# Experts by lists of tokens, weight rows loaded ahead, and the down weights turned inside the attention stage before

## The chip, the cores and the metric

One core of one Trainium2 chip runs the whole program. The metric is device time in microseconds (us); lower is better. The kernel before was timed in three runs.

## The reference, cut to what matters

Two layers, each an attention-like block and a feed-forward block, on `x` of 4 sequences of 512 tokens with 128 features (2048 tokens). The parts that the change touches are the last two: the relative-position attention of the second layer, and its mixture of 8 experts, of which each token uses the one with the largest router logit.

```python
def _L1_ffn_ref(x, router_w, expert_fc, expert_proj):     # E = 8, D = 128, HD = 512
    logits = jnp.einsum('btd,ed->bte', x, router_w)
    probs = jax.nn.softmax(logits, axis=-1)
    expert_ids = jnp.argmax(probs, axis=-1)
    mask = jax.nn.one_hot(expert_ids, E, dtype=x.dtype)
    h = jnp.einsum('btd,edh->ebth', x, expert_fc)
    h = jnp.square(jax.nn.relu(h))
    out_e = jnp.einsum('ebth,edh->ebtd', h, expert_proj)
    return jnp.einsum('ebtd,bte->btd', out_e, mask)
...
x = x + ga * _L1_attn_ref(h, ...)                          # relative attention
h = _layernorm(x, axis=-1) * (1 + cb) + sb
x = x + gb * _L1_ffn_ref(h, L1_ffn_router_w, L1_ffn_expert_fc, L1_ffn_expert_proj)
```

## The kernel before, in words

The program is a row of stages (test-time layer, six transformer layers, relative attention, experts); at the end of each, `end_phase` makes all five engines meet. Inside a stage every engine has its own hand-written order of instructions, and semaphores (`Signal`) tie them: `x.by(event)` raises, `x.on(event)` is waited for. An engine that waits holds everything behind it in its own order. DMAs issued by SP (SyncE) go through one queue, indirect DMAs (row numbers taken from a tile) are issued by POOL (GpSimd), one per 128 rows.

**Relative attention.** 256 tiles of 8 queries are worked through in rounds (`relative_rounds`), two tiles a round: `score_tiles` (L1878, L1884) on PE, the largest score on DVE (L2028), the exponential on ACT (L1996), a turn of the weights by PE one round later (L1899), and a copy of the turned tiles out of PSUM in `relative_keep` (L1952), the even tile on ACT, the odd one on DVE. The next round's scores wait for these copies, since the PSUM banks go round by five. From round 9 on PE also sums the values (L1921, L1931). POOL builds the masked query rows for every four rounds (`make_rows`, L2040 and L2049), and SP fetches them (`fetch_rows`). `t.xc` and `t.hT` of this stage are used only by its early part.

**Experts.** All 2048 tokens are sorted into tiles of 128 that belong to one expert each: `TILES` = 16 + 8 - 1 = 23, of which the last of each expert is partly filled and some may be empty. In order:

- A norm (L256 to L303). Between its two halves PE turns the router and, in `turn_expert` (L2197), all down weights `expert_proj`; DVE and ACT copy them out (L2318, L2279) and SP writes them beside the up weights into a table in memory of 1024 rows of 4 KB (`t.table`). SP also clears `t.sorted`.
- Router logits (L2217), h turned to rows by token (L2221), counts of tokens before each token (`counts_tensor`, L2265 to L2270), the gates (L2225), x turned to rows by token (L2230).
- `places_vector` on DVE (L2360 to L2376): the sorted row of each token (`at_i`), then the weight rows of each tile (`row_i`).
- POOL scatters h into `t.sorted`, 16 indirect DMAs (L2395). SP loads the sorted rows back (L2180). POOL gathers the weights, 23 indirect DMAs of 512 KB into 6 buffers (L2403), each from the seventh on waiting for `downed` of the tile six before.
- The tile loop: PE turns the tile (L2239), up (L2248), relu on DVE (L2338), square on ACT (L2299), down (L2257), copy out on ACT (L2305), store to `t.answers` by SP (L2183).
- When all tiles are stored, POOL gathers the answers back by token, 16 indirect DMAs (L2408); DVE multiplies by the gate and adds x (L2344, L2346) for every four, and SP stores the result (L2187).

The lines that set the order around the change:

```python
G.wait_ge(*t.placed.on(0)); G.wait_ge(*t.zero_in.on(0))
for m in range(NT): ...                      # 16 scatters of h, L2395
for n in range(TILES):
    if n >= WEIGHTS:                         # WEIGHTS = 6
        G.wait_ge(*t.downed.on(n - WEIGHTS))
    G.e.indirect_dma_start(out=t.w[n % WEIGHTS], in_=t.table, ...)     # L2403
for y_out in t.y_out: G.wait_ge(*y_out.all())
for m in range(NT): ...                      # 16 gathers of answers, L2408
```

Of the kernel before, what the change touches and what calls it, by code (L numbers as in the profile page):

```python
# [7 lines left out]
F32 = mybir.dt.float32  # L8
BF16 = mybir.dt.bfloat16
# [153 lines left out]
def setup(nc, io, whole):  # L163
# [8 lines left out]
    c.xT = sbuf(c, whole, "xT", [P, B, S])  # L172
    c.modT = sbuf(c, whole, "modT", [P, 2, 6, B])
# [1401 lines left out]
SPLIT_FROM = len(UNITS) - 2  # L1575
SUM_AT = {"heads": 8, "spread": 8, "out": 8, "turn": 9, "scale": 10, "back": 11, "add": 14, "o_turn": 15, "o_copy": 16, "mix": 16, "bias": 17}
# [197 lines left out]
def relative_late_setup(c, t, scope):  # L1774
# [20 lines left out]
    t.q_made, t.q_high, t.q_low = (Signal(nc, "rel_q_" + n, halves) for n in ("made", "high", "low"))  # L1795
    t.q_shared, t.sums_zeroed = Signal(nc, "rel_q_shared", [0]), Signal(nc, "rel_sums_zeroed", [0])
# [47 lines left out]

def relative_sync(c, t):
# [10 lines left out]
    for signal in (*t.qd_in, *t.o_out.values(), *t.o_in.values()):  # L1856
        SP.wait_ge(*signal.all())
# [30 lines left out]
def relative_tensor(c, t):  # L1888
    PE, psum, ident = c.PE, c.psum, c.ident
    for r, at, valued in relative_rounds():  # L1890
# [4 lines left out]
        if p is not None:  # L1895
            for n in (2 * p, 2 * p + 1):
# [3 lines left out]
                last.then_inc(*t.turned.by(n))  # L1900
        for u, k in valued:
# [33 lines left out]
            if k == SUM_AT["turn"]:  # L1935
# [3 lines left out]
                PE.wait_ge(*t.v_kept.all())  # L1939
# [21 lines left out]
def relative_scalar(c, t):  # L1961
    A = c.A
    for r, at, valued in relative_rounds():
        for u, k in valued:
# [152 lines left out]
LOADS = [range(i, min(i + 4, TILES)) for i in range(0, TILES, 4)]  # L2117
WEIGHTS, UP_LAG, DOWN_LAG = 6, 1, 3


def experts_setup(c, scope):
# [4 lines left out]
    t.table, t.sorted, t.answers = dram("expert_table", (NE * P, 2 * HD)), dram("sorted_tokens", (TILES * P, P)), dram("sorted_answers", (TILES * P, P))  # L2126
# [17 lines left out]
    t.const_in, t.pr_in = Signal(nc, "router_in", range(3), 16), [Signal(nc, f"pr_in{e}", [0], 16) for e in experts]
    t.fc_in, t.pr_out, t.zero_in = Signal(nc, "fc_copied", [0], 16), Signal(nc, "pr_out", experts, 16), Signal(nc, "zeros_in", [0], 16)
    t.zeroed, t.numbered = Signal(nc, "experts_zeroed", [0]), Signal(nc, "experts_numbered", [0])
# [304 lines left out]
```

## Time and profile before

| what | us |
|---|---|
| time, median of 3 runs (lowest, highest) | 2559.96 (2552.66, 2569.27) |
| the profiled execution: its time | 2556.95 |
| the profiled execution: its span | 2555.2 |
| PE busy | 2367.3 (93%) |
| DVE busy | 1749.7 (68%) |
| ACT busy | 1600.4 (63%) |
| POOL busy | 1477.4 (58%) |
| experts stage, from its first instruction to the end of the span | 2415.0 to 2555.2 |

The span goes from the first to the last instruction of the profiled execution; 1.75 us of its time lie outside. Times below are microseconds from the span's start. "Granted clock" is TensorE's clock as a share of its upper level. An engine's idle time costs only where the chain of waits passes through it.

### The profile page before, as it was taken

Reading aid. Unit: us, or ns where it says so; the run is one execution under the profiler, and the core shown is the slowest. Engines: PE = TensorE matmul, PEld = TensorE weight load, DVE = VectorE, ACT = ScalarE, POOL = GpSimd, SP = SyncE. Lnnn points to the kernel's source line nnn. Section 1 sums busy time; section 2 is a strip of 40 time slices with the busy share of each in tenths; the row PEclk is TensorE's granted clock in tenths of the full one; section 3 lists DMA queues with packets and bytes.
Section 4 is the critical chain, followed back from the end, with each engine's and each line's share of the span. In section 5 each row is a group of like instructions: output and inputs, shape, how many; then the busy total and the mean of one; then the engine's idle time right before and its main releaser. Section 6 shows DMA issues by size and latency. Waiting matters only on the chain.

```text
span 2555.2 us, 121984 instructions
## 1 busy us (share of the span) xinstructions
PE 2367.3 (93%) x53661; PEld 1739.5 (68%) x53661; DVE 1749.7 (68%) x3521; ACT 1600.4 (63%) x5055; POOL 1477.4 (58%) x1452
## 2 busy tenths in 40 slices
PE   9858999999999999999999999999889999999855
PEld 8736777777777777777777777777546666666654
DVE  4497887888878888888888877887345555555422
ACT  3226777777777777777777777777534454454322
POOL 1156676666766676667766676664137665566144
PEclk9979999999999999999999999999979999999967
DMA  4013333333333334333343333333132222222255
GB/s 90 14 32 81 80 83 95 91 82 83 94 90 88 85 83 95 93 85 83 93 95 80 86 91 80 89 85 85 36 78 51 47 47 47 48 47 47 69 193 166
DMA packets 234111, 203.55 MB, mean 80 GB/s; under 512 B 133720, under 2 KB 160230, under 8 KB 233454
## 3 DMA queue, kind: packets, MB, share of 16 engines
q1 hardware_dynamic: 227070, 181.28, 29.2%
q0 software_dynamic: 4336, 14.16, 1.7%
q8 instruction: 422, 6.91, 1.2%
q14 instruction: 107, 0.88, 0.1%
q10 hardware_dynamic: 2176, 0.33, 0.1%
HBM read 84.09 MB, written 16.15 MB: 39 GB/s over the span
## 4 chain that ended last, share of the span: by engine, by line
PE 68%; DVE 16%; issue 5%; POOL 3%; SPq 3%; DMA 3%; ACT 2%; POOLq 0%; ACTq 0%; DVEq 0%
PE psum L1197 8%; PE psum L1215 5%; PE psum L1223 5%; PE psum L1899 5%; PE psum L1098 5%; PE psum L1878 4%; PE psum L1884 3%; PE psum L1100 3%; PE psum L1099 3%; PE psum L1931 3%; DVE kT L1430 3%; PE psum L1921 3%; DVE rotated L1405 3%; PE psum L1174 2%; PE psum L1205 2%
## 5 line engine op out<-in xcount | busy, mean ns | idle before, releaser
L1342 ACT ACTIVATE p<-p,stat 128x64 f32<-128x64 f32 x1536 | 512.3, 336 | 38.2 <-DVE stat L1477 36.2
L1560 POOL TENSOR_TENSOR p<-p,inverse 128x512 f32<-128x512 f32 x192 | 200.3, 1043 | 461.6 <-DVE inverse L1480 460.4
L1197 PE MATMUL psum<-kT,qT 32*32 32x64 f32 x24576 | 305.5, 223 | 27.3 <-issue 25.9
L1197 PEld LDWEIGHTS psum<-kT,qT 32*32 32x32 f32 x24576 | 263.5, 103 | 78.1 <-issue 76.8
L2028 DVE TENSOR_REDUCE largest<-psum 128x1 f32<-128x512 f32 x256 | 164.9, 686 | 221.5 <-PE psum L1884 221.5
L1405 DVE SCALAR_TENSOR_TENSOR rotated<-psum,scales,rotary 128x512 f32<-128x512 f32 x384 | 271.5, 742 | 26.3 <-ACT sq L1278 26.0
L1342 ACT ACTIVATION_READ_ACCUMULATOR p<-p,stat 128x1 f32 x1536 | 289.1, 188 | 0.0
L1539 POOL TENSOR_TENSOR sq<-sq 128x512 f32<-128x512 f32 x192 | 245.3, 1277 | 46.6 <-ACT sq L1278 46.5
L1278 ACT ACTIVATE sq<-psum 128x512 f32<-128x512 f32 x384 | 213.0, 582 | 68.6 <-PE psum L1128 52.3
L1952 ACT ACTIVATE w_by_key<-psum 128x512 f32<-128x512 f32 x128 | 76.5, 597 | 245.0 <-PE psum L1899 245.0
L1215 PEld LDWEIGHTS psum<-pT,v_win 64*64 64x64 f32 x12288 | 197.0, 135 | 48.0 <-issue 40.7
L1098 PE MATMUL psum<-xs,wqkv_high 128*128 128x512 f32 x384 | 206.4, 537 | 18.8 <-DVE rotated L1405 13.0
L1215 PE MATMUL psum<-pT,v_win 64*64 64x32 f32 x12288 | 218.4, 220 | 1.8 <-ACT pT L1348 1.4
L1223 PEld LDWEIGHTS psum<-oT,wo 128*128 128x128 f32 x1536 | 187.6, 196 | 41.4 <-issue 30.9
L1223 PE MATMUL psum<-oT,wo 128*128 128x128 f32 x1536 | 198.6, 283 | 12.1 <-issue 6.8
L1348 ACT ACTIVATE pT<-psum 128x512 f32<-128x512 f32 x192 | 114.3, 595 | 140.0 <-PE psum L1205 139.9
L1291 ACT ACTIVATE v_tok<-psum 128x512 f32<-128x512 f32 x192 | 114.0, 594 | 95.7 <-PE psum L1100 79.7
L2040 POOL TENSOR_TENSOR q_by_head<-q_heads,mask_head 64x256 fp32r<-64x256 f32 x252 | 157.4, 624 | 15.4
L1996 ACT ACTIVATE weights<-psum,largest 128x512 f32<-128x512 f32 x256 | 161.5, 687 | 3.5 <-DVE largest L2028 3.5
L1546 POOL TENSOR_TENSOR qT<-qT,rotated 128x512 f32<-128x512 f32 x96 | 162.9, 1697 | 0.0
L1430 DVE TENSOR_TENSOR kT<-kT,rnorm_wide 128x1024 f32<-128x1024 f32 x96 | 157.6, 1642 | 3.5 <-DMA rnorm_wide<-rnorms 3.4
L1405 DVE SCALAR_TENSOR_TENSOR kT<-psum,scales,rotary 128x512 f32<-128x512 f32 x192 | 141.9, 739 | 22.2 <-ACT sq L1278 19.8
(344 smaller groups left out, 5488.2 us busy)
## 6 DMA issues: line engine op xcount, KB each, us to landing
v_win<-v_tok SPq DMA_DIRECT2D x576, 128.0 KB
rnorm_wide<-rnorms SPq DMA_DIRECT2D x384, 64.0 KB
v_win<-v_tok SPq DMA_DIRECT2D x336, 64.0 KB
q_rows<-q_rows_all SPq DMA_DIRECT2D x32, 512.0 KB, 4.7
wqkv<-L_ffn_Wqkv SPq DMA_DIRECT2D x96, 64.0 KB, 2.4
rel_values<-sq SPq DMA_DIRECT2D x60, 64.0 KB, 2.2
wo<-L_ffn_Wo SPq DMA_DIRECT2D x48, 64.0 KB
wqkv<-L_ffn_Wqkv SPq DMA_DIRECT2D x12, 256.0 KB, 2.9
```

Source lines behind the costliest of these rows:

```text
L1098: PE.e.matmul(out, w[0], x[1], start=True, stop=False)
L1197: last = PE.e.matmul(psum[WIN * blk:WIN * (blk + 1), f, out], q[rows, g, half, tok:tok + WIN], k[rows, g, half, tok:tok + 2 * WIN], start= ...
L1215: last = PE.e.matmul(psum[to:to + DH, 2 + o, at:at + WIN], v[rows, blk, 2 * (2 * a + o) + h, :], t.pt[h][rows, 2 * a + o, blk * WIN:(blk + ...
L1223: last = PE.e.matmul(ps[:, 0:P], t.wo[:, e, :], t.ot[e % 2][:, e // 2, :], start=(e == 0), stop=(e == PAIRS - 1))
L1278: A.e.activation(t.sq[half][:, :], c.psum[:, 4 + half, :], ACT.Square).then_inc(*t.squared.by((u, (p, half))))
L1342: last = A.e.activation(p, p, ACT.Exp, bias=t.stat[:, h, 2 * g + f:2 * g + f + 1], accum_out=t.sum[:, h, g, f:f + 1])
L1405: last = V.e.scalar_tensor_tensor(out=rot[x], in0=psum[:, 4 + half, :], scalar=scale, in1=table, op0=ALU.mult, op1=ALU.mult)
L1430: V.e.tensor_tensor(k, k, t.wide[g % 2][:, :].unsqueeze(1).to_broadcast([P, 2, S]), ALU.mult).then_inc(*t.k_scaled.by((u, g)))
L1539: G.e.tensor_tensor(t.sq[0][:, :], t.sq[0][:, :], t.sq[1][:, :], ALU.add).then_inc(*t.squares.by((u, p)))
L1546: G.e.tensor_tensor(second, second, t.turned_by[1][:, :], ALU.add).then_inc(*t.made.by((u, p)))
L1560: G.e.tensor_tensor(p, p, t.inv[:, h, :, :].unsqueeze(3).to_broadcast([P, GROUPS_TF, 2, 2 * WIN]), ALU.mult).then_inc(*t.p_scaled.by(m))
L2028: V.e.tensor_reduce(t.mx[n % 4][:, :], psum[:, n % 5, :], AX, ALU.max, negate=True).then_inc(*t.largest.by(n))
```

## The change

**Relative attention.** The table of weights becomes part of the whole program (`c.table`). SP starts the copy of the up weights into it as its first step of the rounds. In rounds 1 to 8 SP loads the down weights of one expert into `t.xc` (`fetch_weights`), in rounds 4 to 11 PE turns one expert's (four transposes into PSUM bank 7, behind the turn of that round's tiles and ahead of the value sums) and ACT copies it out (ahead of its `relative_keep`), and in rounds 6 to 13 SP stores it (`store_weights`).

**Experts.** The turning and the clearing are gone. Rows of (h, x, gate), 1536 bytes for each of the 2048 tokens and one row of zeros, are written to memory by 13 plain DMAs of SP (`t.rows`). PE makes the gates before it turns h. `places_vector` now makes the weight rows first, and behind the sorted places it makes, with bitwise operations, comparisons and 16 small matmuls (`list_tensor`), a list of token numbers for each tile. SP loads each tile's weights by a plain DMA from a row number that it reads into a register (10 buffers). POOL issues 12 gathers of token rows, then a scatter of a finished tile straight into the output and a gather in turn, then the last 12 scatters; there is no way back over `t.answers`. Gate and x are applied per tile on DVE.

```diff
-WEIGHTS, UP_LAG, DOWN_LAG = 6, 1, 3
+WEIGHTS, LOOK, UP_LAG, DOWN_LAG = 10, 12, 1, 3
+NO_TOKEN = NT * P
...
+def fetch_weights(c, t, e):
+    SP = c.SP
+    SP.wait_ge(*c.norms["normed"].on((2, B - 1)))
+    if e >= 4:
+        SP.wait_ge(*t.pr_turned.on(e - 4))
+    SP.e.dma_start(t.xc[:, e % 4, :], c.io["L1_ffn_expert_proj"][e]).then_inc(*t.pr_in[e % 4].by(e))
...
+def store_weights(c, t, e):
+    SP.wait_ge(*t.pr_kept.on(e))
+    SP.e.dma_start(c.table[e * P:(e + 1) * P, HD:2 * HD], t.hT[:, e % 4, :]).then_inc(*t.pr_out[e % 4].by(e))
...
+def turn_weights_down(c, t, e):
+    PE.wait_ge(*t.v_kept.all())
+    PE.wait_ge(*t.pr_in[e % 4].on(e))
+    if e:
+        PE.wait_ge(*t.pr_kept.on(e - 1))
+    for j in range(TPB):
+        last = PE.e.transpose(c.psum[:, 7, j * P:(j + 1) * P], t.xc[:, e % 4, j * P:(j + 1) * P], c.ident[:, :])
+    last.then_inc(*t.pr_turned.by(e))
...
+def keep_weights_down(c, t, e):
+    A.wait_ge(*t.projected.on((B - 1, "v")))
+    A.wait_ge(*t.pr_turned.on(e))
+    if e >= 4:
+        A.wait_ge(*t.pr_out[e % 4].on(e - 4))
+    A.e.activation(t.hT[:, e % 4, :], c.psum[:, 7, :], ACT.Copy).then_inc(*t.pr_kept.by(e))
...
 def relative_sync(c, t):
+    SP.e.dma_start(c.table[:, 0:HD], c.io["L1_ffn_expert_fc"].rearrange("e d h -> (e d) h")).then_inc(*t.fc_in.by(0))
     for r, at, valued in relative_rounds():
+        if 0 <= r - TABLE_FIRST + TABLE_FETCH < NE:
+            fetch_weights(c, t, r - TABLE_FIRST + TABLE_FETCH)
+        if 0 <= r - TABLE_FIRST - TABLE_LAG < NE:
+            store_weights(c, t, r - TABLE_FIRST - TABLE_LAG)
...
 def experts_sync(c, t):
+    for b in range(B):
+        SP.e.dma_start(part(b, 2), t.gates[:, b:b + 1, :].to_broadcast([P, TPB, P])).then_inc(*t.rows_out.by(("g", b)))
+    for name, kept, source, j in (("h", t.h_kept, t.htok, 0), ("x", t.x_kept, t.xtok, 1)):
+        for b in range(B):
+            SP.wait_ge(*kept.on(b))
+            SP.e.dma_start(part(b, j), source[:, b * TPB:(b + 1) * TPB, :]).then_inc(*t.rows_out.by((name, b)))
+    SP.wait_ge(*t.rowed.on(0))
     for n in range(TILES):
-        SP.wait_ge(*t.y_kept.on(n))
-        SP.e.dma_start(t.answers[n * P:(n + 1) * P, :], t.y[n % 4][:, :]).then_inc(*t.y_out[n % 4].by(n))
+        row = SP.e.value_load(t.row_i[0:1, n:n + 1], min_val=0, max_val=(NE - 1) * P)
+        if n >= WEIGHTS:
+            SP.wait_ge(*t.downed.on(n - WEIGHTS))
+        SP.e.dma_start(t.w[n % WEIGHTS][:, :], c.table[bass.ds(row, P), :]).then_inc(*t.w_in[n % WEIGHTS].by(n))
...
+def list_tensor(c, t):
+    PE, lists = c.PE, c.psum[:, 6, 0:2 * TILES]
+    PE.wait_ge(*t.placed.on(0))
+    for m in range(NT):
+        last = PE.e.matmul(lists, t.in_slot[:, m, :], t.ids[:, m, :, :].rearrange("p j t -> p (j t)"), start=(m == 0), stop=(m == NT - 1))
+    last.then_inc(*t.listed.by(0))
...
 def places_vector(c, t):
-    V.e.tensor_copy(t.at_i[:, :], t.at[:, :]).then_inc(*t.placed.by(0))
+    then(V.e.tensor_copy(t.at_i[:, :], t.at[:, :]))
+    V.e.tensor_scalar(t.slot[:, :], t.at_i[:, :], P - 1, None, ALU.bitwise_and)
+    then(V.e.tensor_scalar(t.base[:, :], t.at_i[:, :], -P, None, ALU.bitwise_and))
+    by_tile = [P, NT, TILES]
+    then(V.e.tensor_tensor(t.in_tile[:, :, :], t.base[:, :].unsqueeze(2).to_broadcast(by_tile), t.tile_at[:, :].unsqueeze(1).to_broadcast(by_tile), ALU.is_equal))
+    V.e.tensor_tensor(t.ids[:, :, 0, :], t.in_tile[:, :, :], t.id_high[:, :].unsqueeze(2).to_broadcast(by_tile), ALU.mult)
+    V.e.tensor_scalar(t.ids[:, :, 1, :], t.in_tile[:, :, :], t.id_low[:, 0:1], None, ALU.mult)
+    by_slot = [P, NT, P]
+    V.e.tensor_tensor(t.in_slot[:, :, :], t.slot[:, :].unsqueeze(2).to_broadcast(by_slot), t.slot_n[:, :].unsqueeze(1).to_broadcast(by_slot), ALU.is_equal).then_inc(*t.placed.by(0))
+    V.wait_ge(*t.listed.on(0))
+    then(V.e.tensor_reduce(t.raw[:, :], psum[:, 6, 0:2 * TILES].rearrange("p (j t) -> p t j", t=TILES), AX, ALU.add))
+    V.e.tensor_scalar(t.token_i[:, :], t.raw[:, :], float(NO_TOKEN), None, ALU.add).then_inc(*t.tokens.by(0))
...
 def experts_vector(c, t):
+            V.e.tensor_tensor(t.y[:, n, :], psum[:, 4 + n % 2, 0:P], t.xs[:, n, 2 * P:3 * P], ALU.mult).then_inc(*t.gated.by(n))
+            V.wait_ge(*t.gated.on(n))
+            V.e.tensor_tensor(t.y[:, n, :], t.y[:, n, :], t.xs[:, n, P:2 * P], ALU.add).then_inc(*t.added.by(n))
...
 def experts_pool(c, t):
+    G.wait_ge(*t.tokens.on(0))
+    G.wait_ge(*t.rows_out.all())
+    out = c.io["out"].rearrange("b s d -> (b s) d")
+    for r in range(TILES + LOOK):
+        n = r - LOOK
+        if n >= 0:
+            G.wait_ge(*t.added.on(n))
+            G.e.indirect_dma_start(out=out, out_offset=bass.IndirectOffsetOnAxis(ap=t.token_i[:, n:n + 1], axis=0), in_=t.y[:, n, :], in_offset=None,
+                                   bounds_check=NO_TOKEN - 1, oob_is_err=False).then_inc(*t.stored.by(n))
+        if r < TILES:
+            G.e.indirect_dma_start(out=t.xs[:, r, :], out_offset=None, in_=t.rows, in_offset=bass.IndirectOffsetOnAxis(ap=t.token_i[:, r:r + 1], axis=0),
+                                   bounds_check=NO_TOKEN).then_inc(*t.xs_in[r % (LOOK + 1)].by(r))
```

## Rows read from the trace of the kernel before

**Rows 1.** the page: the chain that ended last, by engine

```profile
PE 68%; DVE 16%; issue 5%; POOL 3%; SPq 3%; DMA 3%; ACT 2%; POOLq 0%; ACTq 0%; DVEq 0%
```

**Rows 2.** windows: length, busy PE PEld DVE ACT POOL, granted clock, DMA share, GB/s

```profile
2440.00:2442.00 2.00, 2.00 (x11) 2.00 (x12) 1.45 (x5) 0.60 (x1) 0.00 (x0) 0.50 0.03 8
...
2460.00:2480.00 20.00, 4.99 (x22) 4.61 (x23) 1.02 (x2) 1.29 (x4) 13.06 (x14) 0.50 0.52 183
2480.00:2500.00 20.00, 19.77 (x170) 18.86 (x168) 7.29 (x11) 9.60 (x30) 8.98 (x9) 1.00 0.94 297
...
2520.00:2540.00 20.00, 4.02 (x33) 3.72 (x32) 2.84 (x5) 2.04 (x6) 9.84 (x10) 0.70 0.21 58
```

**Rows 3.** groups by line, 2411-2556 us: count, busy us, mean ns, idle before

```profile
L2403 POOL DMA_INDIRECT tile_weights<-expert_table,weight_row_i x23 | 23.1, 1002 | 24.0 <-PE psum L2257 15.6 <-issue 8.3
...
L2408 POOL DMA_INDIRECT y_tokens<-sorted_answers,row_at_i x16 | 16.7, 1043 | 15.9 <-DMA sorted_answers<-tile_y 11.3 <-issue 4.6
...
L2395 POOL DMA_INDIRECT sorted_tokens<-h_tokens,row_at_i x16 | 15.8, 989 | 33.8 <-DVE row_at_i L2370 29.2 <-issue 4.6
...
L2372 DVE TENSOR_TENSOR past<-tile_number,end 128x184 f32<-128x184 f32 x1 | 0.3, 344 | 0.0
```

**Rows 4.** timeline, head of the experts stage: start us, us, engine, line

```profile
2426.29 0.18 DVE L225 SCALAR_TENSOR_TENSOR rstd<-root_t,rstd 128x16 f32<-128x16 f32 x1
...
2432.63 3.74 PE L268 MATMUL psum<-ident,rstd 128*128 128x128 f32 x32
...
2440.22 3.65 PE L2221 MATMUL psum<-ident,hT 128*128 128x128 f32 x16
...
2443.88 1.03 PE L2270 MATMUL psum<-chosen,all_ones 128*128 128x120 bf16 x15
...
2444.77 1.70 PE L2225 MATMUL psum<-ident,gate 128*128 128x128 f32 x8
...
2447.61 0.18 DVE L2370 CAST row_at_i<-row_at 128x16 int32<-128x16 f32 x1
...
2448.71 1.24 POOL L2395 DMA_INDIRECT sorted_tokens<-h_tokens,row_at_i  x1 [29.23 <-DVE row_at_i L2370]
...
2474.76 0.66 PE L2239 MATMUL psum<-ident,sorted_x 128*128 128x128 f32 x2 [26.55 <-DMA sorted_x<-sorted_tokens]
```

**Rows 5.** timeline, end of the experts stage

```profile
2524.70 0.28 ACT L2305 ACTIVATE tile_y<-psum 128x128 f32<-128x128 f32 x1 [0.77 <-PE psum L2257]
...
2539.27 1.52 POOL L2408 DMA_INDIRECT y_tokens<-sorted_answers,row_at_i  x1 [0.30 <-issue]
2539.93 0.69 DVE L2346 TENSOR_TENSOR y_tokens<-y_tokens,x_tokens 128x512 f32<-128x512 f32 x1
...
2547.66 1.01 POOL L2408 DMA_INDIRECT y_tokens<-sorted_answers,row_at_i  x1 [0.30 <-issue]
...
2551.01 0.69 DVE L2346 TENSOR_TENSOR y_tokens<-y_tokens,x_tokens 128x512 f32<-128x512 f32 x1
```

**Rows 6.** timeline, first rounds of the relative attention

```profile
1919.26 0.96 PE L1878 MATMUL psum<-keys,q_by_head 64*128 64x512 f32 x6 [0.25 <-ACT w_by_key L1952]
...
1920.75 1.09 PE L1899 MATMUL psum<-ident,weights 128*128 128x128 f32 x8
...
1921.44 0.60 ACT L1952 ACTIVATE w_by_key<-psum 128x512 f32<-128x512 f32 x1 [1.07 <-PE psum L1899]
...
1922.09 0.96 PE L1878 MATMUL psum<-keys,q_by_head 64*128 64x512 f32 x6 [0.25 <-ACT w_by_key L1952]
...
1929.80 1.04 PE L1878 MATMUL psum<-keys,q_by_head 64*128 64x512 f32 x6 [2.30 <-POOL q_by_query L2049]
...
1934.08 0.97 PE L1878 MATMUL psum<-keys,q_by_head 64*128 64x512 f32 x6
...
1937.83 0.96 PE L1878 MATMUL psum<-keys,q_by_head 64*128 64x512 f32 x6
```

**Rows 7.** the page, DMA issues: KB each, us to landing

```profile
q_rows<-q_rows_all SPq DMA_DIRECT2D x32, 512.0 KB, 4.7
```

More of the change, by code:

```diff
@@ L2144, in experts_setup @@
[L2144 to L2146 removed]
+    t.place, t.at, t.at_i, t.slot, t.base = sb("place", [P, NT, NE]), sb("row_at", [P, NT]), sb("row_at_i", [P, NT], I32), sb("slot", [P, NT], I32), sb("tile_base", [P, NT], I32)
@@ L2160, in experts_setup @@
+    t.turned, t.kept, t.upped, t.relued, t.squared, t.downed, t.gated, t.added = (Signal(nc, "tile_" + n, tiles) for n in ("turned", "kept", "up", "relu", "square", "down", "gated", "added"))
+    t.stored = Signal(nc, "out_stored", tiles, 16, fresh=True)
     t.norm = Norm(c, 3, t.hT, c.xT, t.xc, c.modT[:, 1, 4, :], c.modT[:, 1, 3, :])
@@ L2177, in experts_sync @@
-    SP.wait_ge(*t.scattered.all())
-    for i, tiles in enumerate(LOADS):
-        rows = t.sorted[tiles[0] * P:(tiles[-1] + 1) * P, :].rearrange("(t p) d -> p t d", p=P)
-        SP.e.dma_start(t.xs[:, tiles[0]:tiles[-1] + 1, :], rows).then_inc(*t.xs_in[i].by(0))
-    for n in range(TILES):
-        SP.wait_ge(*t.y_kept.on(n))
-        SP.e.dma_start(t.answers[n * P:(n + 1) * P, :], t.y[n % 4][:, :]).then_inc(*t.y_out[n % 4].by(n))
-    out = io["out"].rearrange("b (c p) d -> p (b c) d", p=P)
@@ L2219, in experts_tensor @@
     for b in range(B):
+        last = PE.e.matmul(psum[:, 7, b * P:(b + 1) * P], c.gate[:, 1, 1, b:b + 1].to_broadcast([P, P]), c.ident[:, :], start=True, stop=True)
+    last.then_inc(*t.gate_out.by(0))
+    for b in range(B):
         for k in range(TPB):
@@ L2224, in experts_tensor @@
     for b in range(B):
-        last = PE.e.matmul(psum[:, 7, b * P:(b + 1) * P], c.gate[:, 1, 1, b:b + 1].to_broadcast([P, P]), c.ident[:, :], start=True, stop=True)
-    last.then_inc(*t.gate_out.by(0))
-    for b in range(B):
         PE.wait_ge(*t.h_kept.on(b))
@@ L2276, in experts_scalar @@
     norm_scalar(c, t.norm)
-    for e in range(1, NE, 2):
-        A.wait_ge(*t.pr_turned.on(e))
-        A.e.activation(t.prT[:, e, :], psum[:, 5, :], ACT.Copy).then_inc(*t.pr_kept[1].by(e))
+    A.wait_ge(*t.gate_out.on(0))
+    A.e.activation(t.gates[:, :, :].rearrange("p b d -> p (b d)"), psum[:, 7, :], ACT.Copy).then_inc(*t.gate_kept.by(0))
     for b in range(B):
@@ L2405, in experts_pool @@
-    for y_out in t.y_out:
-        G.wait_ge(*y_out.all())
-    for m in range(NT):
-        G.e.indirect_dma_start(out=t.ytok[:, m, :], out_offset=None, in_=t.answers, in_offset=bass.IndirectOffsetOnAxis(ap=t.at_i[:, m:m + 1], axis=0),
-                               bounds_check=TILES * P - 1).then_inc(*t.gathered[m // TPB].by(m % TPB))
+        last = G.e.memset(t.up_to[:, e, 0:e + 1], 1.0)
+    last.then_inc(*t.numbered.by(0))
+    G.wait_ge(*t.tokens.on(0))
+    G.wait_ge(*t.rows_out.all())
```

160 lines of the change are left out of this document (59 added, 101 removed).

## The prediction

> **What bounds the kernel now.** I read the chain of waits first. Over the whole span it runs mostly through PE [rows 1], so a stage that keeps PE full pays for every instruction added there. The experts stage is another case, which only windows show: while POOL scatters h, PE is busy 5 of 20 us at granted clock 0.50 (the lower level, 1.2 GHz); while the tiles are worked it is busy 19.8 of 20 at the upper one, with the DMA engines at 0.94; while POOL gathers the answers it is busy 4 of 20 [rows 2]. The groups say why: an indirect DMA holds POOL about 1.0 us and the next comes 0.3 us later. There are 16 + 23 + 16 = 55 of them [rows 3], 16 of them alone before the loop and 16 alone behind it. Last I read the timeline of the stage's two ends [rows 4, 5] and of the attention's first rounds, where work is put in [rows 6].
>
> **Experts, head.** The root of the norm is ready at 2426.47, yet the spread begins at 2432.63, because PE turns the down weights in between [rows 4]. That goes: the spread can begin 6.1 us earlier. PE then starts at its lower clock; I take 0.7 us of the gain back, so the logits end 5.4 us earlier, 2440.2 - 5.4 = 2434.8 (ends: 3 and 6.1). Next on PE came the turn of h (3.65), a short counting part and the counts (together to 2444.9, that is 4.7 after the logits). Now the gates go first, +1.70 [rows 4], so the counts end at 2434.8 + 4.7 + 1.7 = 2441.2. The clock was at its lower level during the turn of h [rows 2]; were it at the upper, this part would be some 2.5 us shorter, which I keep as a bound.
>
> DVE's old way from the counts to `at_i` took 2447.79 - 2444.91 = 2.9 us [rows 4]. Ahead of `at_i` now come the weight rows, three dependent operations: 0.38 + 0.38 + 0.2 = 1.0. Behind it: two bitwise ones of 16 columns, 0.4; then operations of 368, 368, 368 and 2048 columns. From 184 columns at 0.344 [rows 3] and 512 at 0.69 [rows 5] a column costs 1.05 ns over 0.15 us, so 0.54 + 0.54 + 0.54 + 2.3 = 3.9. The list is 16 small matmuls; 15 of the nearest kind took 1.03 [rows 4], so 1.3 with both hand-overs (not above 3). Two more operations, 0.5, and POOL starts 0.92 after DVE's end, as at 2448.71 after 2447.79 [rows 4]. Sum behind the counts: 2.9 + 1.0 + 0.4 + 3.9 + 1.3 + 0.5 + 0.9 = 10.9. POOL's first gather begins at 2441.2 + 10.9 = 2452.1, which is 3.4 us later than its first scatter today. POOL also waits for the 13 plain writes of rows (3 MB). Their last is issued about 5 us behind the counts (turn of x up to 3.7 at the lower clock, 0.6 on ACT). At the 297 GB/s of a full window [rows 2] the 3 MB take 10.6 us from 2437.4, where the gates are ready, so about 2449 and 2 us of landing: just covered. If they are slower by 2 us, they set the start.
>
> **Experts, loop and end.** POOL now issues 23 gathers and 23 scatters: 46 against 55. The gather's price per start is 1.0 + 0.3 = 1.31 us for 512 KB as for 64 KB, the scatter's 1.28 [rows 3, 4]; so size does not matter and 1536 bytes a row should cost 1.31 too. From the first start to the last: 23 x 1.31 + 22 x 1.28 = 58.3 us. That POOL sets the pace needs a comparison with the tiles. Tile 0 today is finished 8 us after its first turn, and all 23 take 2524.98 - 2474.76 = 50.2 us [rows 4, 5]. With 3.5 us for the first gather's landing, tile 22 is added about 54.5 us after POOL's start, the last scatter begins 58.3 after it, and the first at 12 x 1.31 = 15.7 against tile 0's 12. POOL is late by 4 us at both ends, so PE's loop is hidden under POOL and not the other way. DVE takes two more operations of 0.3 per tile and ACT loses one of 0.26; both have free time [rows 2].
>
> The last scatter lands 2.5 us after its start (DVE's work on the last gather begins that much behind 2547.66 [rows 5]) and the span ends 0.3 later. So the span would end at 2452.1 + 58.3 + 2.8 = 2513.2, not at 2555.2: 42.0 us earlier. Gone are the 16 scatters ahead (20 us), the reload (6), the 16 gathers behind (21) and the way out (8); come back 3.4 at the start and the loop's stretch from 50 to 61.
>
> SP's plain weight loads hide here: the weight rows are known 2441.2 + 3.9 = 2445, the h and x writes are ahead of them on SP until 2446, and ten buffers are filled before POOL's first gather needs any. The trace has no register load on SP. I bound it by nothing and by a transfer's 4.7 us from issue to landing [rows 7]; I take 1 us, as nearest to a DMA issue, and below 2 us a tile it is hidden.
>
> **Attention.** Rounds 4 to 7 cost 2.83 us each: scores at 1919.26, the turn at 1920.75, ACT's copy at 1921.44 for 0.60, the next scores at 1922.09 [rows 6]. The new step is not free beside this, since the next scores wait for that copy and ACT now first copies the weights: the turn of eight (1.09) ends, four more (0.43) follow, then ACT 0.6 + 0.6. The next scores come 1.49 + 1.09 + 0.43 + 1.20 + 0.1 = 4.3 after the last ones, +1.5 a round, +5.9 for four. Round 8 waited for POOL, 2.3 us until 1929.80, of which about 2.0 take up the delay: +3.9. Round 8 itself lasted 4.3 (PE had cooled) and has that chain too: +0. Rounds 9 to 11 lasted 3.75 with the value sums on PE; the same chain gives 1.95 + 1.09 + 0.43 + 1.20 + 0.1 = 4.8, +1.0 each, +3.0. Sum +7 us (ends: +2 if most of it fits under POOL's wait, +17 if the gaps of 1.3 us put PE at its lower clock, where round 8 showed 4.3 in place of 2.8). PE is full in the later rounds, so nothing absorbs this. SP's row fetches go behind the weight stores but are needed rounds later; the 2 MB copy runs when DMA has room.
>
> **Sum.** 2555.2 - 42.0 + 7.0 = 2520.2 of span, 2522.0 of time against the profiled 2556.95. That execution is 3 us under the median of 2559.96, so against the median: 2525.
>
> **A rule weighed.** One gather of the answers took 1.52 us where its neighbours took 1.01; DVE ran an addition of two SBUF tiles beside it (2539.93) [rows 5]. The others beside such additions took no longer. The Trainium skill (SBUF — State Buffer, Who interferes with whom) says that a DVE instruction with two SBUF inputs blocks a GpSimd instruction that reads SBUF, though it also infers that descriptor generation needs the other interface. By that rule the new additions on DVE would hold POOL up; what it would do is the third rival.
>
> **Rivals.**
> 1. *The transfers set the loop.* 23 x (512 + 192 KB) + 1 MB = 17.6 MB must move after 2446. Windows show 297 GB/s at share 0.94 [rows 2]: 59 us, last load at 2505, and 8 us more: 2513, as in the forecast. It speaks against me that rows of 1.5 KB and scatters may move slower; at 250 GB/s the loads end at 2516 and the stage at 2524, 11 us later: 2536.
> 2. *The attention pays double*: PE falls to its lower clock in rounds 4 to 8. For: it did so after 2.3 us of waiting. Against: gaps of 1.3 us are shorter. +17 in place of +7: 2535.
> 3. *DVE holds POOL.* 23 additions times the one observed 0.51: +12: 2537. Against: three of four such meetings cost nothing.
> 4. *Less cost than I think*: the attention's delay mostly covered (+2) and the head at the upper clock (-2.5), no other change: 2517 or somewhat below.
> 5. *Slower.* The pace is POOL's, so if an indirect DMA with numbers out of range, or with a dozen outstanding, holds POOL for x us, the stage grows by 46 (x - 1.3). All the gain of 35 is gone at x = 2.06; at 2.2 the time is 2566. For: no row shows either condition. Against: all 23 weight gathers took about 1.0 at DMA share above 0.9.
> That the change does nothing it says is hardly possible: nine indirect DMAs and both solitary stretches go by construction.
>
> **Chances.** Forecast 0.45; rival 1 0.18; rival 2 0.14; rival 3 0.11; rival 4 0.08; rival 5 0.04. A measurement of this kernel tells about 1%, 26 us, from no change, so the line is at 2534. Forecast and rival 4 are beyond it (0.53), the first three rivals lie around it and give 0.28 (they can be partial), in all 0.81 faster. Slower by over 1% needs rival 5 in full: 0.03. The rest, 0.16, is within 1%. The range goes from rival 4 with the scatter of the runs, 2508, to rivals 1 to 3 with it, 2546.
>
> **What would show it.** Right: POOL issues 46 indirect DMAs of about 1.0 us without a wait for DVE after the twelfth, the last near 2517; the spread right behind the root; rounds 4 to 7 at 4.3 us. Wrong: POOL waiting for `added`, PE waiting for weights or rows in the loop, a mean over 1.2 us for an indirect DMA, or rounds 9 to 11 unchanged.

## The result, and the profile after

The kernel after takes 2547.6 us (median of five, 2544.6 to 2548.6), the kernel before 2561.9 beside it: ratio 0.9943, interval [0.9922, 0.9965], 14 us less. The forecast was 2525 with a range up to 2546. The profiled execution has a span of 2545.8 us. I divide it at the first product of the last norm (L257), where the experts stage starts, and at POOL's indirect transfers; "before" and "forecast" are divided in the same way.

| part of the span, us | before | forecast | after |
|---|---|---|---|
| up to the scores of the attention's first round | 1904.9 | 1904.9 | 1912.8 |
| from there to the start of the experts stage | 510.1 | 517.1 | 516.1 |
| stage start to POOL's first indirect transfer | 33.7 | 37.1 | 38.6 |
| POOL's first to its last start | 99.0 | 58.3 | 73.2 |
| last start to the end | 7.5 | 2.8 | 5.1 |
| span | 2555.2 | 2520.2 | 2545.8 |

The first line is code that the change doesn't touch; over the traces of this study it lies between 1893.7 and 1916.1. So the time of a single execution says little here, and the stretches below are compared in place of it. Of the 25.6 us missed in this execution it has 7.9, the stretch of POOL's transfers 14.9.

The groups of the loop after, by line, from 2462 to 2546 us (columns as in [rows 3]); those of before are [rows 3]:

```profile
L2437 POOL DMA_INDIRECT tile_rows<-token_rows,token_list x23 | 24.0, 1044 | 43.8 <-DVE token_list L2409 37.1 <-issue 6.7
L2434 POOL DMA_INDIRECT out<-tile_y,token_list x23 | 23.2, 1009 | 20.2 <-DVE tile_y L2370 13.1 <-issue 7.1
L2364 DVE TENSOR_SCALAR relu<-psum 128x512 f32<-128x512 f32 x23 | 15.8, 689 | 32.7 <-issue 12.8 <-PE psum L2275 11.7 <-remote 8.2
```

Read the POOL lines first. One transfer costs 1.04 and 1.01 us, about as forecast, but the scatters waited 13.1 us for DVE's last addition of a tile (L2370): the tiles, and not POOL, were late. The third line shows that it wasn't DVE: its relu stood idle before its turn, and for 8.2 us of that a semaphore was raised just before the relu while no instruction had ended near that time ("remote"); "issue" is idle time in which the engine waited for nothing that the profile shows.

The timeline shows one such place. Columns: start, duration, engine, line, operation, and the idle time before it with its releaser:

```profile
2491.29 1.13 PE L2275 MATMUL psum<-tile_hT,tile_weights 128*128 128x128 f32 x8
...
2492.25 1.06 PE L2284 MATMUL psum<-tile_weights,square 128*128 128x128 f32 x8
2493.15 0.27 PE L2266 MATMUL psum<-ident,tile_rows 128*128 128x128 f32 x1
...
2496.75 0.29 DVE L2368 TENSOR_TENSOR tile_y<-psum,tile_rows 128x128 f32<-128x128 f32 x1 [2.21 <-remote]
...
2498.15 0.28 ACT L2326 ACTIVATE tile_hT<-psum 128x128 f32<-128x128 f32 x1 [2.95 <-remote]
...
2498.52 2.05 PE L2275 MATMUL psum<-tile_hT,tile_weights 128*128 128x128 f32 x8 [5.11 <-ACT tile_hT L2326]
2499.53 1.04 POOL L2437 DMA_INDIRECT tile_rows<-token_rows,token_list  x1 [0.30 <-issue]
2499.71 0.69 DVE L2364 TENSOR_SCALAR relu<-psum 128x512 f32<-128x512 f32 x1 [2.34 <-remote]
```

Which end belongs to which reader has to be counted out, since each of these groups has one member a tile, 23 in all, and each engine takes the tiles in order (tile 0 first). The relu at 2499.71 is that of tile 7, whose eight products of L2275 end at 2492.4 by TensorE's own record (the first line): 7.3 us between them. The eight products of L2284 that end at 2493.3 are tile 5's and are read at 2501.19, 7.9 us later; DVE's start at 2496.75 is for tile 4, whose products ended at 2491.2. ACT's copy at 2498.15 is of tile 8, turned by 2491.3, 6.8 us before. Only then can TensorE go on with tile 8: 5.11 us idle, after which its products take 2.05 us in place of 1.06 (granted clock 0.57 from 2498 to 2502). I call these late completions.

In this loop relu starts over 0.5 us late in 11 of 23 tiles; in the loop of before it starts within 0.1 us of TensorE's end in all 23. The semaphore events recorded in the trace are late too, so it isn't the readers that hang back: 31 of them come more than 0.5 us after the last recorded end of any instruction that raises that semaphore, all 31 are TensorE's and in this loop, and the trace of before has none. Since TensorE's ends are modelled, the trace doesn't tell whether the products themselves were late or only their signals.

The granted clock and the transfers, by windows (columns as in [rows 2]). In the full window of the loop of before TensorE was busy 19.8 of 20 us at clock 1.00 [rows 2]:

```profile
2440.00:2460.00 20.00, 18.66 (x121) 18.36 (x121) 9.44 (x27) 4.80 (x9) 0.00 (x0) 0.66 0.29 87
...
2467.00:2485.00 18.00, 9.16 (x54) 8.66 (x54) 2.09 (x4) 2.77 (x7) 12.55 (x12) 0.61 0.97 368
2485.00:2525.00 40.00, 28.54 (x218) 27.60 (x219) 16.61 (x42) 11.22 (x27) 24.39 (x24) 0.91 0.75 235
```

After 2485 the DMA engines are at 0.75 and no engine is full. TensorE has 28.5 us of work in 40.

The attention's rounds show what was forecast. Round 4 begins at 1924.33, round 5 at 1928.58:

```profile
1924.33 0.96 PE L1922 MATMUL psum<-keys,q_by_head 64*128 64x512 f32 x6 [0.30 <-issue]
...
1925.81 1.09 PE L1943 MATMUL psum<-ident,weights 128*128 128x128 f32 x8
...
1926.74 0.60 PE L1871 MATMUL psum<-ident,xc 128*128 128x128 f32 x4
...
1927.44 0.60 ACT L1881 ACTIVATE hT<-psum 128x512 f32<-128x512 f32 x1 [2.05 <-PE psum L1871]
1927.93 0.59 ACT L1998 ACTIVATE w_by_key<-psum 128x512 f32<-128x512 f32 x1
...
1928.58 0.98 PE L1922 MATMUL psum<-keys,q_by_head 64*128 64x512 f32 x6 [1.24 <-ACT w_by_key L1998]
```

### The profile page after: what moved, and what is told of

Same layout as the page of the kernel before. It is cut to its first block, busy times and chain, and to the rows that moved or that the text cites. A ratio compares the mean times of both kernels' runs of the same rounds, so it can differ in the third digit from the quotient of the medians.

```text
span 2545.8 us, 122108 instructions
## 1 busy us (share of the span) xinstructions
PE 2377.6 (93%) x53677; PEld 1751.0 (69%) x53677; DVE 1759.1 (69%) x3561; ACT 1599.6 (63%) x5036; POOL 1464.2 (58%) x1408
## 4 chain that ended last, share of the span: by engine, by line
PE 72%; DVE 18%; issue 4%; ACT 2%; POOL 1%; SPq 1%; DMA 1%; another core or an unknown queue 0%; POOLq 0%; ACTq 0%; DVEq 0%
PE psum L1198 8%; PE psum L1216 6%; PE psum L1224 5%; PE psum L1943 5%; PE psum L1099 5%; PE psum L1922 5%; PE psum L1928 4%; PE psum L1101 4%; PE psum L1100 3%; DVE kT L1431 3%; PE psum L1977 3%; PE psum L1967 3%; DVE rotated L1406 3%; PE psum L1175 3%; PE psum L1206 2%
## 5 line engine op out<-in xcount | busy, mean ns | idle before, releaser
L1099 PE MATMUL psum<-xs,wqkv_high 128*128 128x512 f32 x384 | 206.7, 538 | 18.8 <-DVE rotated L1406 12.9
L1406 DVE SCALAR_TENSOR_TENSOR kT<-psum,scales,rotary 128x512 f32<-128x512 f32 x192 | 141.9, 739 | 22.2 <-ACT sq L1279 19.8
```

Source lines behind the costliest of these rows:

```text
L1099: PE.e.matmul(out, w[0], x[1], start=True, stop=False)
L1406: last = V.e.scalar_tensor_tensor(out=rot[x], in0=psum[:, 4 + half, :], scalar=scale, in1=table, op0=ALU.mult, op1=ALU.mult)
```

## Experiments

There were 18 runs: three of the kernel after unchanged (b0, c1, e3) and 15 of eleven edited kernels, nine of these runs with a single execution. The question was what makes the tile loop late; the second was whether the attention's price can be saved. "Stretch" is always the time from POOL's first to its last start; "gap" the time from one relu to the next (1.9 us is TensorE's work for a tile: 8 + 8 products and a turn). The chips are numbered as in the results; the run of the result above has no number.

**Fewer buffers, gathers first, fewer loads (chip 4).**

```diff
-WEIGHTS, LOOK, UP_LAG, DOWN_LAG = 10, 12, 1, 3
+WEIGHTS, LOOK, UP_LAG, DOWN_LAG = 6, 12, 1, 3      (a1)
+WEIGHTS, LOOK, UP_LAG, DOWN_LAG = 10, 22, 1, 3     (a2)
-    for n in range(TILES):
+    for n in range(WEIGHTS):                       (a3, loads)
```

> The kernel after, with six weight buffers in place of ten (as many as before had). Theory A, late completions of TensorE come from the burst of ten 512 KB weight loads at the head of the loop: with six in the burst, POOL's first gather lands earlier than 7 us after its issue, and the 73.2 us from POOL's first to its last start shrink by up to 10 us. Theory B, the loop is slow for another reason (the row gathers or the scatters beside the tiles): 73 us stays within 3, or grows because weights now come only six tiles ahead. The time: 2540 by A, 2547 to 2552 by B.

> The kernel after, with all but one of POOL's 23 gathers ahead of the first scatter (22 in place of 12). If a gather queued behind a scatter that waits for its tile is what holds the tiles up (theory C: POOL waits for the addition, then the next gather is late, then TensorE waits), TensorE never waits for rows after the first tiles and the loop is over some 10 us earlier: 2538. If TensorE and not the rows sets the pace (theories A and B), the last scatter starts where it does now, within 3 us, and the time is 2547; the first scatters come some 13 us later, at no cost.

> The kernel after, with only the first ten of the 23 weight loads; each later tile takes the weights that its buffer holds already (this part of the computation is changed). Theory A2, the weight loads in the loop (and the register loads on SP with them) cause TensorE's late completions: the lags of 1 to 3.5 us between TensorE's last product of a tile and DVE's relu go for tiles after the tenth, POOL's first to last start falls from 73 to about 60 us. Theory B, row gathers and scatters cause them: the lags stay and the 73 us within 4.

a1: 0.9931 [0.991, 0.9952], stretch 74.2. a2: 0.9946 [0.9931, 0.9962], stretch 74.1. a3: 2533.2 us in its one run, stretch 71.4. Neither the burst of ten loads, nor the order of gathers and scatters, nor the later loads make the loop late: theories A, A2 and C fell. (The times of a1 and a2, 2535.5 and 2538.8 us, lie below the 2547 that theory B gave, a2's even where theory C had it; but the kernel before is 8 us faster on this chip too, at 2553.6.) But a2's timeline gave the first hint:

```profile
2472.20 1.13 PE L2275 MATMUL psum<-tile_hT,tile_weights 128*128 128x128 f32 x8 [0.34 <-issue]
...
2473.17 1.06 PE L2284 MATMUL psum<-tile_weights,square 128*128 128x128 f32 x8
...
2474.06 0.27 PE L2266 MATMUL psum<-ident,tile_rows 128*128 128x128 f32 x1
...
2480.66 1.91 PE L2284 MATMUL psum<-tile_weights,square 128*128 128x128 f32 x8
2482.37 0.42 PE L2266 MATMUL psum<-ident,tile_rows 128*128 128x128 f32 x1
...
2486.19 0.69 DVE L2364 TENSOR_SCALAR relu<-psum 128x512 f32<-128x512 f32 x1 [7.15 <-remote]
2486.91 0.63 ACT L2332 ACTIVATE square<-relu 128x512 f32<-128x512 f32 x1 [8.19 <-DVE relu L2364]
2487.09 1.05 POOL L2437 DMA_INDIRECT tile_rows<-token_rows,token_list  x1 [0.31 <-issue]
2490.41 0.29 DVE L2368 TENSOR_TENSOR tile_y<-psum,tile_rows 128x128 f32<-128x128 f32 x1 [3.53 <-remote]
2490.45 0.28 ACT L2326 ACTIVATE tile_hT<-psum 128x128 f32<-128x128 f32 x1 [2.90 <-remote]
```

Counted by tile, the relu at 2486.19 reads tile 3's products, recorded as over at 2473.3; DVE's next (2490.41) reads tile 1's, over at 2474.2, and ACT's copy (2490.45) reads tile 5's turn, over at 2474.3: 12.9, 16.2 and 16.1 us. The signals of the last two are recorded at 2490.4. After 2490.6 no signal of TensorE is late. POOL's first 24 starts came one upon the other until 2487.09, then it waited for tiles; from the relu at 2490.95 on all eighteen gaps are 1.8 to 2.3 us, with scatters going on. So something that POOL did without a pause, up to there, seems to hold the completions back.

**Plain row loads (chip 4).**

```diff
+        SP.e.dma_start(t.xs[:, n, :], t.rows[n % NT * P:(n % NT + 1) * P, :]).then_inc(...)   # in SP's loop
-            G.e.indirect_dma_start(out=t.xs[:, r, :], out_offset=None, in_=t.rows, ...)
```

> The kernel after, with the rows of a tile loaded by SP in one plain transfer of 128 neighbouring rows (not the tile's own tokens: this part of the computation is changed), so that POOL only scatters. Theory B, the indirect gathers cause TensorE's late completions: these go, and the loop is as fast as the tiles of the kernel before, about 2.2 us each, POOL's last scatter some 55 us behind the token list. Theory A2, the weight loads cause them: the lags stay, the last scatter 65 us or more behind the token list.

Measured: 2516.7 us. DVE's relu no longer has a "remote" wait and starts within 0.1 us of TensorE's end in all 23 tiles, and POOL's 23 scatters come at the pace of the tiles:

```profile
L2368 DVE TENSOR_SCALAR relu<-psum 128x512 f32<-128x512 f32 x23 | 15.9, 692 | 19.4 <-PE psum L2279 19.0 <-issue 0.4
L2438 POOL DMA_INDIRECT out<-tile_y,token_list x23 | 22.6, 981 | 71.2 <-issue 70.9 <-DVE tile_y L2374 0.3
```

The gap is 1.9 us from the fifth relu on, with the DMA engines full (the view gives a share of 1.04 from 2470 to 2500). The last scatter starts 56.7 us behind the token list. POOL's gathers are in the cause.

**A false trail: the one no-token row (chip 13).** 2944 slots stand for 2048 tokens, so 896 gathers of a row go to the same row.

```diff
+    then(V.e.tensor_scalar(t.empty[:, :], t.raw[:, :], 0.0, t.id_low[:, 0:1], ALU.is_ge, ALU.mult))
-    V.e.tensor_scalar(t.token_i[:, :], t.raw[:, :], float(NO_TOKEN), None, ALU.add)...
+    V.e.scalar_tensor_tensor(out=t.token_i[:, :], in0=t.raw[:, :], scalar=float(NO_TOKEN), in1=t.empty[:, :], op0=ALU.add, op1=ALU.add)...   (a5)
-in_offset=bass.IndirectOffsetOnAxis(ap=t.token_i[:, r:r + 1], axis=0)
+in_offset=bass.IndirectOffsetOnAxis(ap=t.order_i[:, r:r + 1], axis=0)     (a6)
-out=t.xs[:, r, :], out_offset=None, in_=t.rows
+out=t.xs[:, r, 0:P], out_offset=None, in_=t.h_rows                        (a7)
```

> The kernel after, with 128 no-token rows in place of one: slot p of a tile that has no token reads row p of them, at the price of one more small operation on DVE ahead of the first gather (0.3 us). Theory B1, the many reads of one and the same row of DRAM (2944 slots for 2048 tokens, so 896 of them) hold up the DMA engines and with them TensorE's completions: the loop runs at the 1.9 us a tile that stood alone where POOL issued no gathers, and POOL's first to last start falls from 73 to 60 us, the time to 2530. Theory B2, the gathers do it whatever row they read: the 73 us stay within 3.

> The kernel after, with POOL's gathers reading rows in order (row p + 128 n, from a constant list) in place of the tile's tokens (this part of the computation is changed): the same number and size of indirect transfers, but no row read twice in one and neighbours read together. Theory B1 or one in which scattered addresses matter: 1.9 us a tile and POOL's stretch 60 us. Theory B2, the indirect gathers themselves: as the kernel after, 70 us or more.

> The kernel after, with POOL's gathers bringing only h, 512 bytes a row in place of 1536 (DVE multiplies and adds h in place of the gate and x, so this part of the computation is changed). Theory B3, the bytes of the rows beside the weights are what is too much: a third of them, and the loop runs at about 2 us a tile, POOL's stretch near 60 us. Theory B2, the number of indirect transfers counts and not their bytes: 70 us or more.

a5: 0.9897 [0.9881, 0.9914], stretch 60.0, gaps of 1.9. a6: 2516.8 us, stretch 60.6. a7: 2514.8, stretch 60.4. I took this for proof of theory B1, though a7, which still reads the one row, spoke against it. What none of the three had was the kernel after beside it.

**The kernel after again (chip 0), the rows spread another way, and ACT's copy moved.**

```diff
+        p = at(TURN_LAG)
+        if p is not None:
+            relative_keep(c, t, 2 * p)
         if 0 <= r - TABLE_FIRST < NE:
             keep_weights_down(c, t, r - TABLE_FIRST)
-        p = at(TURN_LAG)
-        if p is not None:
-            relative_keep(c, t, 2 * p)           (b1, on top of a5)
-    then(V.e.tensor_scalar(t.empty[:, :], t.raw[:, :], 0.0, t.id_low[:, 0:1], ALU.is_ge, ALU.mult))
+    then(V.e.tensor_scalar(t.empty[:, :], t.raw[:, :], 0.0, None, ALU.is_ge))
+    then(V.e.tensor_tensor(t.empty[:, :], t.empty[:, :], t.tile_n[:, :], ALU.mult))     (a8)
```

> The kernel after, unchanged, as the neighbour of the two that follow on the same chip. Whatever the theory: 0.9943 of before within 0.002, POOL's stretch from first to last start between 70 and 76 us, since it was 73 to 74 in the three kernels that left the one no-token row as it was.

> Spread no-token rows, and ACT's copy of the turned weights placed behind its copy of w_by_key in the same round, in place of ahead of it. Theory D, the order on ACT is what makes rounds 4 to 11 longer (the next scores wait for the copy of w_by_key): rounds 4 to 7 go back from 4.2 to 2.9 us, round 8 waits for POOL again and takes 2 us of this back, rounds 9 to 11 gain 0.6 each: 5 us less than with the spread rows alone, ratio 0.988. Theory E, four more matrix products and a fuller TensorE queue are the price: rounds stay above 3.8 us and the ratio at 0.990.

> The no-token rows spread the other way: tile n's empty slots all read row n of them, so that rows are shared within one gather but never between two. If the many reads of one row inside one gather are what stops TensorE's completions (theory F): lags come back where a tile has many empty slots, POOL's stretch 65 to 74 us. If the reads of one row by a dozen outstanding gathers together are needed (theory G): 1.9 us a tile and a stretch of 60 us, as with 128 rows.

b0 refuted its expectation: the unchanged kernel has a stretch of 60.9 here, gaps of 1.9, and 0.9895 [0.9867, 0.9923]. Its groups, to be held against those of the first profile after:

```profile
L2437 POOL DMA_INDIRECT tile_rows<-token_rows,token_list x23 | 24.1, 1048 | 44.6 <-DVE token_list L2409 37.9 <-issue 5.5 <-DVE tile_y L2370 1.2
L2434 POOL DMA_INDIRECT out<-tile_y,token_list x23 | 23.5, 1021 | 7.5 <-issue 6.3 <-DVE tile_y L2370 1.2
L2364 DVE TENSOR_SCALAR relu<-psum 128x512 f32<-128x512 f32 x23 | 15.9, 692 | 21.4 <-PE psum L2275 21.4
```

The wait for additions is 1.2 us where it was 13.1, and "remote" is gone, with the same instructions; relu starts within 0.1 us of TensorE's end in all 23 tiles, in each of the six traces of chips 0 and 13. a8 (2531.0 us, stretch 60.1) tells nothing more on such a chip. b1: 0.9844 [0.9822, 0.9866], stretch 60.2.

**Side by side (chip 4 again).**

> The kernel after once more, unchanged. So far its loop was drawn out (73 us from POOL's first to last start, gaps of 3 to 7 us between relus) in the run with the result and, with one edit each, on the chip of the first experiments, and undisturbed (61 us, 1.9 us a tile) on the chip of the last ones. Theory H, it is the chip that decides: this run is like one of the two, in all its times alike (0.989 or 0.994 of before).

> The kernel with 128 no-token rows, directly beside the kernel after on the same chip. Theory B1, the one no-token row draws the loop out where the chip lets it: if the kernel after shows 70 us or more here, this one shows 60. Theory H alone, the row has nothing to do with it: both are drawn out, or both are not. If the kernel after is undisturbed here, this pair says nothing between the two and both take 60 to 61 us.

c1: 0.9941 [0.992, 0.9962], stretch 71.9. c2: 0.9942 [0.992, 0.9964], stretch 74.0. Both are late, so theory B1 fell, and the one row has no part in it. Theory H stands, that the chip decides, though it is not fully shown: chip 4 was late in both of its sessions, but every other chip had one session only, so the hour could do the same. The times of the kernel before don't tell the two kinds apart (medians 2550.4 to 2558.9 us on the late chips, 2550.7 and 2558.6 on the others).

**Order and bytes on a chip of that kind (chip 12).** The edits are those of a6, a7 and b1.

> As a6_rows_in_order, for a chip on which the loop is drawn out (the neighbour d3 tells whether this one is). Theory I, it is the scattered rows that POOL's gathers read: read in order, the loop runs at 1.9 us a tile and POOL's stretch is 60 us. Theory J, indirect gathers of any rows do it: 70 us or more. On a chip that does not draw the loop out the run tells nothing between the two.

> As a7_gather_h_only, for a chip on which the loop is drawn out. If the bytes of the gathers decide (theory B3), a third of them leaves the loop at 1.9 to 2.1 us a tile and the stretch at 60 to 63 us; if their number or their scattered rows do, it stays at 70 us or more.

> The kernel b1_copy_behind again, as the neighbour of d1 and d2 and for its time on a second chip. If the chip draws the loop out, POOL's stretch is 70 to 75 us and the ratio to before 0.989 (0.994 less the 5 us of the attention's rounds); if not, 60 us and 0.984 to 0.988.

d3 has a stretch of 76.3 and gaps up to 6.6, so the chip is one of that kind. d1 has 74.5 with rows in order (2544.3 us), d2 has 75.6 with a third of the bytes (2553.4 us, of which the untouched first part has 11 more than in the trace of before). Theories I and B3 fell; J and B2 held. d3: 0.9939 [0.992, 0.9958], where 0.989 was expected. Its rounds of the attention:

```profile
1917.14 0.96 PE L1922 MATMUL psum<-keys,q_by_head 64*128 64x512 f32 x6 [0.30 <-issue]
...
1919.32 0.60 ACT L1998 ACTIVATE w_by_key<-psum 128x512 f32<-128x512 f32 x1 [1.12 <-PE psum L1943]
1919.56 0.60 PE L1871 MATMUL psum<-ident,xc 128*128 128x128 f32 x4
...
1920.09 0.96 PE L1922 MATMUL psum<-keys,q_by_head 64*128 64x512 f32 x6
1920.25 0.60 ACT L1881 ACTIVATE hT<-psum 128x512 f32<-128x512 f32 x1 [0.33 <-PE psum L1871]
```

The copy of w_by_key comes first, the scores follow it 2.95 us after the last ones (4.2 in the kernel after), and the copy of the weights falls beside them. From the scores of round 0 to those of round 12 it is 40.2 us in d3 and 42.3 in b1 (where round 7 took 5.2 us, as it took 4.9 before), 46.3 in the kernel after and 40.4 before: theory D, with 4 to 6 us. Rounds 4 to 6 went back to about 2.95 us as expected; rounds 9 to 11 gained 0.2 each (4.2 against 4.4), not 0.6.

**Is it gathers, or any indirect transfer? (chip 2).** Both kernels are a4 with 23 more indirect transfers where the gathers stood:

```diff
+            G.e.indirect_dma_start(out=t.spare, out_offset=bass.IndirectOffsetOnAxis(ap=t.token_i[:, r:r + 1], axis=0), in_=t.htok[:, r % NT, :], ...)   (e1)
+            G.e.indirect_dma_start(out=t.spare[:, r, :], out_offset=None, in_=t.rows, in_offset=bass.IndirectOffsetOnAxis(ap=t.token_i[:, r:r + 1], axis=0), ...)   (e2)
```

> As a4_plain_rows (rows by plain transfers, this part of the computation is changed), with 23 more scatters on POOL, of h into a spare tensor, in the very places where the gathers stood: 46 indirect transfers as in the kernel after, none of them a gather. Theory K, POOL's indirect transfers back to back do it on a chip that draws the loop out: lags of 1 to 6 us between relus come back, POOL's stretch is 70 us or more. Theory L, only gathers do it: 1.9 us a tile, 60 us.

> As a4_plain_rows, with the 23 gathers of the kernel after still issued, into a spare tile that nobody reads (this part of the computation is changed, and 4.5 MB more are moved). Theories K and L: on a chip that draws the loop out the lags come back though no tile depends on a gather, 70 us or more. Theory M, the lags are the tiles' own waiting for gathered rows: 1.9 us a tile, 60 us.

> The kernel after, as the neighbour of e1 and e2: POOL's stretch tells which kind of chip this is, 70 us or more on one that draws the loop out (and 0.994 of before), 61 us on one that does not (0.989).

e3: 0.9947 [0.9925, 0.997], stretch 75.6, so chip 2 is of that kind too. e1: 2541.7 us, stretch 75.7; e2: 2540.5 us, stretch 77.7. In e1 there isn't one gather, and no tile depends on the added transfers; yet:

```profile
L2444 POOL DMA_INDIRECT spare_rows<-h_tokens,token_list x23 | 22.6, 983 | 44.6 <-DVE token_list L2416 37.9 <-issue 6.7
L2441 POOL DMA_INDIRECT out<-tile_y,token_list x23 | 22.3, 971 | 25.0 <-DVE tile_y L2377 17.4 <-issue 7.6
L2371 DVE TENSOR_SCALAR relu<-psum 128x512 f32<-128x512 f32 x23 | 15.8, 687 | 30.9 <-remote 14.1 <-issue 12.0 <-PE psum L2282 4.8
```

"Remote" is at 14.1 us, with gaps up to 8.6. Gaps of up to 3.4 us go on behind the last spare transfer at 2512.6, where the scatters still come in groups of two or three. Theory K: indirect transfers that POOL issues back to back (one each 1.3 us) hold TensorE's completions up; 23 of them at a tile's pace don't (a4, and the tail of a2). a4 ran on chip 4 and not beside e1 and e2; what ties them is that the kernel after is late on both chips.

## Why the prediction was wrong

The stretches of all kernels with 46 transfers fall into two groups with nothing between, whatever the edit:

| chip | stretch, us | ratio of the kernel after |
|---|---|---|
| of the result | 73.2 | 0.9943 |
| 4 | 74.2, 74.1, 71.4, 71.9, 74.0 | 0.9941 |
| 12 | 74.5, 75.6, 76.3 | |
| 2 | 75.7, 77.7, 75.6 | 0.9947 |
| 0 | 60.9, 60.2, 60.1 | 0.9895 |
| 13 | 60.0, 60.6, 60.4 | |

**The step that failed** is "POOL is late by 4 us at both ends, so PE's loop is hidden under POOL". The stretch was 73.2 us where 58.3 were forecast. On chips 4, 12 and 2, and in the run of the result, TensorE's loop, held up by its late completions, came out on top, and POOL waited for it. It took TensorE's pace from the loop of before, where it was not disturbed; that loop had one indirect transfer a tile, and [rows 2] has beside full TensorE work only 9 transfers in 20 us (2480 to 2500). The change itself makes that stretch. None of the five rivals had this mechanism; rival 1 had the place (the loop) and nearly the size (11 us, against 12.3 between this stretch and the 60.9 of chip 0), but the windows above refute its cause. That the forecast missed its range by only 1.6 us is no sign that the account was nearly right: the head and the rounds came out close, the loop did not. The sign that was to show it, "POOL waiting for `added`", did.

Where the chip doesn't do this, the loop's term stood nearly in full: a stretch of 60.9 in b0 against 58.3, of which 2.4 are the two kinds of wait for an addition in the groups above. The time of b0 is 26 us below that of before beside it (2532.3 against 2558.6), where 35 were forecast; head (+2.3), stretch (+2.6), tail (+2.2) and attention (-1.1) account for 6 of the 9, and the other 3 stay open.

Point by point, on the profiled execution:

- *Head, spread 6.1 us earlier, 0.7 given back to the clock.* The spread did follow the root at once, but from there to the end of the logits it was 10.7 us against 7.6 before: TensorE came out of a pause and ran mostly at the lower clock (granted clock 0.66 from 2440.8 to 2451.5, against 0.93 before, where the turning filled the pause). 3.1 given back in place of 0.7. This term was mis-sized.

```profile
2440.56 0.17 DVE L226 SCALAR_TENSOR_TENSOR rstd<-root_t,rstd 128x16 f32<-128x16 f32 x1
2440.79 6.75 PE L269 MATMUL psum<-ident,rstd 128*128 128x128 f32 x32 [2.40 <-DVE rstd L226]
...
2451.55 0.29 DVE L2345 COPY logits<-psum 128x128 f32<-128x128 f32 x1 [2.71 <-PE psum L2244]
...
2463.05 2.28 DVE L2406 TENSOR_TENSOR in_slot<-slot,slot_number 128x2048 bf16<-128x2048 int32 x1
2465.39 0.79 PE L2306 MATMUL psum<-ids_by_tile,in_slot 128*128 128x46 bf16 x16 [5.93 <-DVE in_slot L2406]
...
2467.56 1.27 POOL L2437 DMA_INDIRECT tile_rows<-token_rows,token_list  x1 [37.09 <-DVE token_list L2409]
```

- *From the counts to the first gather 10.9 us.* Measured 9.9, from 2457.65 to 2467.56: the wide comparison 2.28 (2.3 forecast), the list 0.9 with both hand-overs (1.3 forecast). The writes of rows did not set the start. Right.
- *Indirect transfers at the old price*: right, so rivals 3 and 5 are refuted. On the rule weighed: an addition of DVE with two SBUF inputs ran beside 16 of the 46; these took 1.02 us on average, the other 30 took 1.03. On chip 0 it was 22 of 46, with 1.04 and 1.03.
- *First gather lands after 3.5 us*: the first tile's turn (L2266) began 7 us after the issue. The ten weight loads in flight aren't the reason shown: with six it was 6.7 us (a1). It cost little, since POOL still had gathers to issue.
- *Tail 2.8*: the span ended 5.1 us after the start of the last scatter to `out`, in every run but a4 (3.3); 2.5 was the price of a gather.
- *Attention +7.0*: +5.9 (46.3 against 40.4 from round 0 to round 12). Rounds 4 to 7 took 4.2 to 4.4 us (4.3 forecast), 9 to 11 took 4.4 (4.8 forecast); the last three are where the forecast was too high. Rival 2 is refuted, and the reason given, ACT's copy of the weights ahead of the one that the scores wait for, is shown by b1 and d3.
- *What is gone*: the prediction's list of 20, 6, 21 and 8 us adds up to 55; its rows give 56.3, and the forecast of 42.0 goes by the rows.

**What stays open.** The runs tie the late completions to POOL's indirect transfers back to back and, as far as one session a chip can, to the chip. By what path the one reaches the other isn't shown, nor is it whether the kernel before, with one transfer a tile, has a little of it on such chips: its one trace has no chip number. A loop with POOL's transfers further apart wasn't tried.

**The version with the copy behind**: b1 (spread rows and the copy behind) has 0.9844 on chip 0, 13 us below the kernel after beside it (2519.5 against 2532.3). The spread rows alone gave nothing (c2 0.9942 beside c1 0.9941). The trace accounts for 4 us of that by the rounds, the rest is scatter of the executions or not explained. On chips with late completions it shows no gain: 0.9939 on chip 12, against 0.9941 to 0.9947 for the kernel after on others, though its rounds were shorter there too.

## What to carry to other kernels

Before an engine's loop is called hidden under another's, ask whether the change makes the other one do something that the trace of before never showed beside it, here indirect transfers one upon the other beside full TensorE work; put the loop's price with that in the range. And if two runs of the same code disagree by more than their scatter, run the unchanged kernel beside each edit on the same chip before a cause is believed: three edits seemed to cure what the chip didn't have.

## What the runs showed of the hardware

On three of five numbered chips and in the run of the result, while POOL issued an indirect transfer each 1.3 us, readers on DVE and ACT started up to 7.9 us after TensorE's recorded end (16.2 in a2), TensorE's semaphore events came late, those of no other engine did, and a stretch of 60 us became one of 71 to 78; two chips showed nothing of it. With 23 transfers at a tile's pace it was absent too (a4). The readers' own work kept its length (relu 689 ns against 692). The Trainium skill (SBUF — State Buffer, Who interferes with whom) has as its single rule that only the port pair shared by DVE and GpSimd causes contention, and TensorE isn't on it. The runs differ from this if it is read as "GpSimd's transfers never slow TensorE"; whether SBUF has any part in it they don't show.
